# A fused attention and feed-forward kernel: two PSUM banks exchanged in the down products, and no read of a state that is zero

## The reference

```python
x  = L0_attn_x                                   # (8, 1024, 512)
xn = _layernorm(x)
# attention, for i in range(3): k, v are 128 wide
w = decay ** maximum(diff - 1, 0) * (diff > 0)
scores = einsum('btd,bsd->bts', q, k) * w
blended += softmax(xn @ Wg)[..., i:i+1] * einsum('bts,bsd->btd', scores, v)
s = blended @ Wo * out_scale
# feed-forward, inner width 1376, weights looked up in a table of 16 values
g = silu((silu(xn @ gate.T) * (xn @ up.T)) @ down.T)
x + s * g
```

## Time and profile before

| what | value |
|---|---|
| median of 3 runs | 1904.91 us (1904.81 to 1905.32) |
| profiled execution, its own time | 1905.76 us |
| its span, first to last instruction | 1903.9 us |
| PE busy | 1849.9 us, 97% of the span |
| DVE busy | 1230.2 us, 65% |
| ACT busy | 648.5 us, 34% |
| POOL busy | 643.0 us, 34% |
| mean busy share of the 16 DMA engines' queue q1 | 52.9% |
| mean granted clock of TensorE | 0.995 of full speed |

### The profile page before, as it was taken

The page is one execution under the profiler, slowest core; times in us unless marked ns, Lnnn a source line. Parts: engine busy times, 40 slices in busy tenths (PEclk is TensorE's granted clock), DMA queues, the critical chain, the costliest instruction groups (busy, mean ns, idle before and its releaser), DMA issues.

```text
span 1903.9 us, 39485 instructions
## 1 busy us (share of the span) xinstructions
PE 1849.9 (97%) x14214; PEld 1250.5 (66%) x14214; DVE 1230.2 (65%) x2589; ACT 648.5 (34%) x1168; POOL 643.0 (34%) x642
## 2 busy tenths in 40 slices
PE   5899999999999999999999999999999999999999
PEld 1236758485775848576685858667584867758485
DVE  7785848485674848476584847658484856748374
ACT  2563334142333414233342324233241424334131
POOL 9301606043250605234160613416061432506021
PEclk9999999999999999999999999999999999999999
DMA  9984736365563735455472645547363655637350
GB/s 211 308 219 134 185 89 184 99 159 133 151 163 99 195 87 161 132 155 152 110 198 75 171 130 153 139 127 192 81 178 107 160 138 140 173 95 195 68 139 26
DMA packets 353020, 276.73 MB, mean 145 GB/s; under 512 B 220349, under 2 KB 257600, under 8 KB 352752
## 3 DMA queue, kind: packets, MB, share of 16 engines
q1 hardware_dynamic: 341888, 267.61, 52.9%
q0 software_dynamic: 10944, 6.50, 2.4%
HBM read 204.16 MB, written 30.54 MB: 123 GB/s over the span
## 4 chain that ended last, share of the span: by engine, by line
PE 57%; POOL 19%; issue 14%; ACT 4%; DVE 3%; SPq 1%; DMA 1%; POOLq 0%; ACTq 0%; DVEq 0%
PE F L1565 24%; PE B L1425 15%; PE F L1536 11%; POOL region L693 4%; POOL region L686 4%; POOL xhat_half L709 2%; POOL region L698 2%; ACT region L761 2%; DVE region L999 1%; PE B L1456 1%; POOL tt L722 1%; POOL tt L720 1%; POOL chalf L726 1%; POOL tt L717 1%; POOL faded L703 1%
## 5 line engine op out<-in xcount | busy, mean ns | idle before, releaser
L1536 PE MATMUL F<-xtc,ring 128*128 128x256 f16 (+1 forms) x4224 | 497.7, 273 | 0.0
L1536 PEld LDWEIGHTS F<-xtc,ring 128*128 128x128 f16 (+1 forms) x4224 | 416.1, 100 | 42.3
L1565 PE MATMUL F<-wd_hi,region 128*128 128x512 f16 (+1 forms) x1408 | 429.4, 379 | 8.5 <-ACT region L874 8.5
L1536 PE MATMUL F<-xt,ring 128*128 128x256 f16 (+1 forms) x3168 | 378.7, 273 | 0.3
L1536 PEld LDWEIGHTS F<-xt,ring 128*128 128x128 f16 (+1 forms) x3168 | 310.0, 100 | 36.0 <-DVE region L1257 2.1
L1565 PE MATMUL F<-wd_lo,region 128*128 128x512 f16 (+1 forms) x704 | 266.7, 379 | 0.0
L1565 PEld LDWEIGHTS F<-wd_hi,region 128*128 128x128 f16 (+1 forms) x1408 | 137.5, 98 | 175.2 <-ACT region L874 12.6
L1341 DVE SCALAR_TENSOR_TENSOR region<-F,row_out,region 128x512 f32<-128x512 f32 x64 | 48.0, 751 | 302.5 <-ACT region L926 302.5
L680 POOL TENSOR_TENSOR rstd<-var,nhalf 128x4 f32<-128x4 f32 x15 | 15.1, 1010 | 650.5 <-DVE var L957 650.5
L926 ACT ACTIVATE region<-F,scale_hf 128x512 f32<-128x512 f32 x64 | 44.0, 688 | 446.8 <-PE F L1565 446.8
L686 POOL TENSOR_TENSOR region<-region 128x512 f16<-128x512 f32 x96 | 118.1, 1231 | 220.8 <-ACT region L761 220.8
(11 more groups left out here) (197 smaller groups left out, 2972.1 us busy)
## 6 DMA issues: line engine op xcount, KB each, us to landing
ring<-blocks SPq DMA_DIRECT2D x546, 256.0 KB, 3.1
x_sb<-in_x SPq DMA_DIRECT2D x64, 256.0 KB, 3.7
out_y<-x_sb SPq DMA_DIRECT2D x64, 256.0 KB, 2.0
ring<-blocks SPq DMA_DIRECT2D x112, 128.0 KB, 2.5
blocks<-ring SPq DMA_DIRECT2D x35, 256.0 KB, 7.2
x_sb<-codes SPq DMA_DIRECT2D x10, 512.0 KB, 8.7
chalf<-codes SPq DMA_DIRECT2D x9, 512.0 KB, 8.7
xt<-codes SPq DMA_DIRECT2D x9, 512.0 KB, 9.4
```

Of the source, the lines that this page charges most:

```text
L1536: ins = T_.matmul(out_, a, b, start=fresh, stop=False, skip_group_check=True)
L1565: ins = T_.matmul(bf[:, :], a, b, start=(k == 0 and n == 0), stop=(k == FC - 1 and n == 2))
```

## The change

Three things change.

1. In the down products of even tiles (d = 0 and 2) the banks are exchanged: the down product goes to `FB[1]` and the attention output to `FB[0]`. The first down product of a group now waits for `u2` of the last set instead of `silu1`, and the attention output behind it for `silu1`. The readers on ACT and DVE and the first two products of the next group follow suit.
2. For the first tile of a sequence (n = 0 and g = 0) PE leaves out the fp32 matmul with the state.
3. For the same tile DVE leaves out the three terms of `B[2]` and raises the semaphore by the three steps itself.

```diff
@@ ACT, behind the products of a group
-                    nc.scalar.activation(g_sb[:, d % 2], FB[(0, 3)[d % 2]][:, :], ACT.Silu,
+                    nc.scalar.activation(g_sb[:, d % 2], FB[(1, 3)[d % 2]][:, :], ACT.Silu,
@@ DVE, mix
+                if n == 0 and g == 0:
+                    dve.wait_ge(s_mix, c0 + NH)
+                    dve.sem_inc(s_mix, NH)
+                    return
                 for h in range(NH):
                     dve.wait_ge(s_mix, c0 + NH + h)
                     V_.scalar_tensor_tensor(out=acc, in0=B[2][:, h * D:(h + 1) * D], scalar=gate_t[:, t, h:h + 1],
@@ DVE, behind the products
-                    V_.scalar_tensor_tensor(out=g_sb[:, d % 2], in0=FB[(1, 2)[d % 2]][:, :], scalar=row_out[:, t:t + 1],
+                    V_.scalar_tensor_tensor(out=g_sb[:, d % 2], in0=FB[(0, 2)[d % 2]][:, :], scalar=row_out[:, t:t + 1],
@@ PE, retrieve
-                pe.wait_ge(s_st, gi * GT + n + 1)
-                T_.matmul(B[2][:, 0:HD], q32[:, cols], state[:, :], start=True, stop=True)
+                if n or g:
+                    pe.wait_ge(s_st, gi * GT + n + 1)
+                    T_.matmul(B[2][:, 0:HD], q32[:, cols], state[:, :], start=True, stop=True)
@@ PE, product
-                        pe.wait_ge(*((s_sg1, q) if s else (s_g, gi * GT + FREE)))
+                        pe.wait_ge(*((s_sg1, q) if s else (s_y1, gi * GT + FREE)))
                     elif p == 1:
-                        pe.wait_ge(*((s_u2, q) if s else (s_y1, gi * GT + FREE)))
+                        pe.wait_ge(*((s_u2, q) if s else (s_g, gi * GT + FREE)))
@@ PE, down products
-                    bf, bs = FB[(0, 3)[d % 2]], FB[(1, 2)[d % 2]]
+                    bf, bs = FB[(1, 3)[d % 2]], FB[(0, 2)[d % 2]]
                     elif d == 0:
-                        pe.wait_ge(s_sg1, gi * NSET + NSET)
+                        pe.wait_ge(s_u2, gi * NSET + NSET)
...
                     elif d == 0:
-                        pe.wait_ge(s_u2, gi * NSET + NSET)
+                        pe.wait_ge(s_sg1, gi * NSET + NSET)
```

More of the change, by code:

```diff
@@ L1139, in softmax_out, with mix @@
                                  fade_q[:, :].unsqueeze(1).broadcast_to([P, GT, NH]), ALU.mult).then_inc(s_sm, 1)
-            def mix(gi, n):
+            def mix(gi, g, n):
                 t = DOWN[n]
@@ L1313, in group @@
                     if n in MIX:
-                        mix(gi, MIX[n])
+                        mix(gi, g, MIX[n])
                     if n in ROWS1:
@@ L1335, in group @@
                         update_state(i, g, GT - 1)
-                        mix(gi, GT - 1)
+                        mix(gi, g, GT - 1)
                         rows1(gi, GT - 1)
```

## The result

| | before | after |
|---|---|---|
| median of the runs, us | 1904.86 (4 runs, 1903.39 to 1905.32) | 1886.82 (4 runs, 1886.13 to 1889.16) |
| the profiled execution, us | 1905.76, span 1903.9 | 1886.13, span 1884.3 |
| ratio after to before | | 0.9904, 95% interval 0.9892 to 0.9916 |

By the ratio the change wins 18.3 us (16.0 to 20.6 by the interval); the two medians differ by 18.0. The forecast was 1886.8. Its first two terms are borne out, the third is not, though the total hides that.

What follows compares the result with a forecast made beforehand. PE, busy 1849.9 of 1903.9 us, was taken as the bound. 11.2 + 5.2 + 1.7 = 18.1 us off the median of 1904.91 gave 1886.8 us, with a range of 1885.0 to 1893.0.

Steps and rivals of the forecast that it cites:

- first two terms: On PE, 11.2 us from exchanging banks before the down products and 5.2 us from leaving out eight state matmuls.
- the third: DVE's three terms less, to close PE's wait before p = 5 in seven first groups: 1.7 us.
- The banks: PE's wait for `silu1` before the first down matmul goes in all 16 groups: 11.2 us.
- the profile's 8.5: The profile's own idle time before the down products, taken as the bank exchange's lower bound: 8.5 us.
- the exchange starts nothing earlier: Something unseen beside `silu1` holds the first down matmul until about 223.99: 1898.0 us, 4 in 100.
- What is late next: In the earlier down phase, the nearest input, POOL's `h_lo` of the last set, keeps 3.45 us of slack.
- The state matmul: PE's matmul at the first retrieval costs 0.65 us in each of 8 sequences: 5.2 us.
- The gap before p = 5: PE's 0.24 us wait for `u4` of the last set closes in the loop's seven first groups: 1.7 us.
- the gap before p = 5 stays: Rival: the chain to `u4` may be set by a step following PE, not the mixing: 1888.5 us, 20 in 100.
- DVE and POOL meet elsewhere: Rival: moving DVE makes a new meeting with POOL in the chain to `u4`, 0.83 us: 1892.6 us, 5 in 100.

Runs made afterwards that it cites:

- e1: The kernel before with only the banks exchanged, without the change's two other parts: 1894.99 us, ratio 0.9942.
- e4: The kernel before with only the banks exchanged, but PE's wait for `silu1` put back ahead of the first down matmul: 1906.7 us, ratio 1.0005.
- e7: The kernel after with POOL's `x_sums_low(1)` put ahead of its last steps of the group, its last operation repeated twice: 1913.4 us.
- e8: The kernel before with every state matmul issued twice, 64 more: 1946.06 us, ratio 1.0207.
- e3: The kernel before with only DVE's three terms left out, PE keeping the state matmul: 1904.83 us, ratio 0.9992.
- e11: The kernel after with POOL's line 703 for a sequence's second tile held until DVE's `u2` of the third set is done: 1885.7 us.
- e2: The kernel before without the first tile's state matmul and DVE's three terms, banks not exchanged: 1900.58 us, ratio 0.9969.
- e12: The kernel before with its hardware loops written out on all five engines: 1898.21 us, ratio 0.9958.
- e9: The kernel after with its hardware loops written out on all five engines: 1879.28 us, ratio 0.9860.

## Why the prediction was right, and where it was not

- **The banks, 11.2 us: right.** The passages went from 11.2 to 0.1 us, e1 alone gives 11.0, and e4 takes all of it back with the one wait. The choice of 11.2 over the profile's 8.5 was right too, by the rows and not by the medians: the idle time that the profile lists counts from a matmul's modelled end and left out 0.16 us per group. The rival that the exchange starts nothing earlier is out.
- **What is late next: nothing, right.** `h_lo` of the last set has the 3.45 us left that were forecast, and e7 shows what happens past it.
- **The state matmul, 5.2 us: right.** 0.65 us in its place after, 0.645 each in e8.
- **The gap before p = 5, 1.7 us: this step failed.** "The chain is moved up by up to 1.0 us, PE by 0.65, so it gains 0.35 on PE, more than the 0.24 that it lacks" holds neither at the chain's start nor at its end. 0.2 us of 1.7 came. The sum took PE's 0.65 off the chain's 1.0, but DVE's steps ahead of the mixing follow PE and came 0.65 earlier with it, so the two add: `c12` of the second set starts 1.50 us earlier in the first group (20.74, now 19.24), 0.85 of it against PE's products, and as much in e3 with PE unmoved. Then the chain lost part of it to a wait for PE at `u2`, and the rest where DVE's step fell behind POOL's line 703. e3 shows that the terms alone do this, e11 that this one meeting decides it.
- **The rivals.** The outcome is "the gap before p = 5 stays". Its reason was given as a chain that follows PE. That is the part up to `u2`, but not what decides; the cause is that of the other rival, "DVE and POOL meet elsewhere", at a smaller price: 0.50 us (0.80 to 1.30), not 0.83. Together with what the chain had gained it comes to nearly zero, not to 4.1 us of loss. The Trainium skill's rule (SBUF — State Buffer, Who interferes with whom) says that the second of the two waits for the whole of the first, and by that rule the order of start decides. The traces agree: 0.74 us when DVE is first, 1.30 when it is second, and then it ends 0.55 us after POOL's step. The 0.74 us that the prediction called "alone" was such a step, with POOL 0.13 us behind it; the price is the same.
- **The total.** By the trace the edits gave 11.1 + 5.2 + 0.2 = 16.5 us; e1 and e2 add up to 16.9. The measured 18.3 (16.0 to 20.6) holds that sum. In the profiled pair the start-up and the turns of the loop gave the other 3 us, and both vary without any edit. Where the loop is written out (e12 and e9) the rows count 18.5 us and 18.7 are measured. So the point forecast for the median was met to 0.1 us with one term wrong, by chance. Why those two vary, none of the kernels shows.

## What to carry to other kernels

When the engine that bounds a kernel passes from one phase to the next, look at which buffer its first instruction overwrites: if it is the one whose reader is last in the phase before, exchanging two buffers with a pair whose readers were done earlier costs no instruction and takes the wait away in every iteration. Read such waits from start to start, as the listed idle time can be too small. A step taken off an engine that isn't the bound is worth nothing until the whole chain from it to the bound has been followed, and with DVE and POOL in that chain the order in which they start, here by under 0.1 us, can cost what was left of the step saved.

## What the runs showed that I had not expected

- **The turn of the loop.** The profile books it as "issue", 3.0 us for PE in the kernel after, but written out the kernel is 7.5 us faster after (e9) and 8.1 before (e12, 1906.33 to 1898.21). The loop turns six times, between its seven passes. Counted from start to start, the two pauses of PE are 0.5 to 1.2 us a turn after, 4.8 in all, and 0.9 to 1.1 a turn before, 6.3 in all; e9 and e12 have neither. After, the gap before p = 5 adds 1.4. Before, it adds 1.7, but the 14 passages grow from 0.68 to 0.83, which takes 2.1 back. Why a passage is longer where the code is written out, no run shows.
- **0.06 us decide 0.5 us, either way.** DVE first by 0.06 us took 0.74 (327.24, above). In the third sequence of the kernel after, POOL's step begins at 621.70 and DVE's at 621.76, and DVE's takes 1.31:

```profile
621.70 0.82 POOL L703 TENSOR_TENSOR faded<-state,fade_tile 128x384 f32<-128x384 f32 x1
...
621.76 1.31 DVE L1293 SCALAR_TENSOR_TENSOR region<-region,scale_hf 128x512 f32<-128x512 f32 x1
```

- **A wait without a releaser.** In e4 9.2 us of waiting for ACT are labelled "issue". A wait in the program on an engine whose data the instruction doesn't touch is not found by the profile's names. The chain of e4 shows PE at 93%, as if nothing held it, though PE's passages add up to 11.9 us there.
